# Graph attention on one core: DVE turns half of the mask tiles of the last two row chunks, and ACT and POOL take over the sums at two borders

## The reference

```
h  = maximum(layernorm(x), 0)                # x [4096, 128]
Wh = h @ W;  a1, a2 = a[:128, 0], a[128:, 0]
e  = (Wh @ a1)[:, None] + (Wh @ a2)[None, :]
e  = where(e > 0, e, 0.2 * e)
e  = where(adj > 0, e, -9e15)                # adj [4096, 4096] int32, 64 MB
out = x + elu(softmax(e, axis=1) @ Wh)
```

## Time and profile before

| | |
|---|---|
| time, median of 3 runs (lowest to highest) | 244.91 us (244.35 to 244.97) |
| profiled execution: its own time, its span | 244.79 us, 243.0 us |
| busy share of the span: PE, PEld, DVE, ACT, POOL | 93%, 91%, 81%, 64%, 24% |
| granted TensorE clock, mean | 0.982 of full speed |
| DMA: moved, mean rate | 71.92 MB, 296 GB/s |

### The profile page before, as it was taken

The page is one execution under the profiler, slowest core; times in us unless marked ns, Lnnn a source line. Parts: engine busy times, 40 slices in busy tenths (PEclk is TensorE's granted clock), DMA queues, the critical chain, the costliest instruction groups (busy, mean ns, idle before and its releaser), DMA issues.

```text
span 243.0 us, 8254 instructions
## 1 busy us (share of the span) xinstructions
PE 227.0 (93%) x3736; PEld 221.2 (91%) x3736; DVE 196.4 (81%) x259; ACT 156.2 (64%) x139; POOL 59.1 (24%) x48
## 2 busy tenths in 40 slices
PE   6969999599999999999999999999999999999970
PEld 2759899599998999999999999999999999999970
DVE  4999997536776998889887988898879888998864
ACT  3698836697799999944996677019975774000051
POOL 3648036897000070300000560000001710040000
PEclk9997999999999999999999999999999999999995
DMA  6999999999998999999999999999999300020002
GB/s 225 360 389 386 386 386 385 388 367 370 301 352 284 363 395 386 388 385 385 398 386 385 388 385 385 385 387 369 386 386 386 140 0 3 3 89 3 3 0 92
DMA packets 36521, 71.92 MB, mean 296 GB/s; under 512 B 1282, under 2 KB 1924, under 8 KB 36484
## 3 DMA queue, kind: packets, MB, share of 16 engines
q1 hardware_dynamic: 35520, 69.74, 79.0%
q10 hardware_dynamic: 964, 1.64, 1.8%
HBM read 69.27 MB, written 2.10 MB: 294 GB/s over the span
## 4 chain that ended last, share of the span: by engine, by line
PE 74%; ACT 8%; DVE 7%; issue 4%; POOL 4%; DMA 1%; ACTq 0%; DVEq 0%; POOLq 0%
PE acc L834 20%; PE acc L835 20%; PE acc L836 20%; PE mask_t L817 11%; ACT mask L420 4%; POOL v L330 2%; POOL val L333 2%; ACT neg L432 1%; DVE words L610 1%; DVE stats L547 1%; DMA x_sb<-in_x_dram 1%; PE acc L796 1%; PE acc L805 1%; ACT neg L511 1%; DVE wh_sb L573 1%
## 5 line engine op out<-in xcount | busy, mean ns | idle before, releaser
L610 DVE SCALAR_TENSOR_TENSOR words<-g_row,gq_word,mask_t 128x1024 f32<-128x1024 f32 x128 | 161.4, 1278 | 36.0 <-PE acc L836 19.0
L834 PE MATMUL acc<-val,words 128*128 128x129 f16 x1000 | 171.9, 220 | 0.3 <-DVE wh_sb L573 0.3
L835 PE MATMUL acc<-val,words 128*128 128x129 f16 x1000 | 171.9, 220 | 0.0
L836 PE MATMUL acc<-val,words 128*128 128x129 f16 x1000 | 171.9, 220 | 0.0
L420 ACT ACTIVATE mask<-raw,step_bias 128x2048 uint8<-128x2048 int32 x63 | 121.8, 1993 | 28.4 <-DVE x_sb L626 17.3
L834 PEld LDWEIGHTS acc<-val,words 128*128 128x128 f16 x1000 | 97.8, 98 | 0.5 <-issue 0.5
L835 PEld LDWEIGHTS acc<-val,words 128*128 128x128 f16 x1000 | 97.9, 98 | 0.1
L836 PEld LDWEIGHTS acc<-val,words 128*128 128x128 f16 x1000 | 97.8, 98 | 0.0
L817 PE MATMUL mask_t<-ident_b,mask 128*128 128x128 bf16 x512 | 34.3, 221 | 1.8 <-ACT mask L420 1.8
L817 PEld LDWEIGHTS mask_t<-ident_b,mask 128*128 128x128 bf16 x512 | 30.3, 99 | 2.2 <-ACT mask L420 2.2
L358 POOL TENSOR_TENSOR hp<-num,rz 128x1024 f32<-128x1024 f32 x3 | 5.7, 1897 | 105.3 <-DVE rz L621 105.3
(11 more groups left out here) (91 smaller groups left out, 125.4 us busy)
## 6 DMA issues: line engine op xcount, KB each, us to landing
raw<-in_adj_dram SPq DMA_DIRECT2D x64, 1024.0 KB, 14.1
x_sb<-in_x_dram SPq DMA_DIRECT2D x8, 256.0 KB, 5.7
out_dram<-x_sb ACTq DMA_DIRECT2D x3, 512.0 KB, 7.9
out_dram<-x_sb SPq DMA_DIRECT2D x2, 128.0 KB, 2.4
out_dram<-x_sb SPq DMA_DIRECT2D x1, 192.0 KB, 1.9
w_sb<-in_L_gnn_W_dram ACTq DMA_DIRECT2D x1, 64.0 KB
out_dram<-x_sb SPq DMA_DIRECT2D x1, 64.0 KB, 1.6
a_sb<-in_L_gnn_a_dram ACTq DMA_DIRECT2D x1, 1.0 KB
```

Source lines behind the costliest of these rows:

```text
L610: nc.vector.scalar_tensor_tensor(words[:, q], g_row[:, c * CHUNK:(c + 1) * CHUNK], gq_word[:, 1, t:t + 1], maskt_bytes[:, u % 2, q // 2, : ...
L834: nc.tensor.matmul(acc_tile(t), high, val[:, tile, 0, 0:V], start=first and t % PT == 0, stop=False, skip_group_check=True)
L835: nc.tensor.matmul(acc_tile(t), high, val[:, tile, 1, 0:V], start=False, stop=False, skip_group_check=True)
L836: last = nc.tensor.matmul(acc_tile(t), low, val[:, tile, 0, 0:V], start=False, stop=False, skip_group_check=True)
```

## The change

**DVE turns.** In chunks 2 and 3 the columns of units 4 to 7 (columns 2048 to 4095, here called a set) go another way. A set's 1024 x 2048 numbers come in four loads of 2 MB; load h holds 256 rows of it. A quarter of the partitions (32) holds these rows with 512 of the columns, so a load is four DMAs of 512 KB, each to 32 partitions: SP issues those of quarters 0 and 1, and ACT those of quarters 2 and 3 (`load_set` on both). ACT makes bytes of them into pair buffers (`set_to_bytes`), and one DVE instruction, `transpose` of 128x1024 words of four bytes in squares of 32, turns a unit (`turn_set`). It writes `mask_t` in a layout in which a byte of four belongs to each q. The 16 transposes on PE fall away for these eight units. DVE turns a unit ahead of the last step of the unit before.

**Order.** In these chunks the units run in the order 0, 1, 4, 2, 5, 3, 6, 7, and the loads in the order unit 0, set load 0, set load 1, unit 1, set loads 2 and 3, units 2 and 3 (`LOADS`). Unit 4, in third place, needs all four set loads. `mask` has two slots in these chunks, as the other two are a pair buffer.

**Values.** The columns of a turned set lie on other partitions, so SP moves the value tiles of the second half with 16 DMAs of 80 KB from SBUF to SBUF (`move_values`, four behind each of loads 18 to 21). DVE writes the word of each column beside the value tiles (`split_weights_sums`, two small copies more), and POOL clears that space once at the start. Row tiles of chunks 2 and 3 are in linear order; their rows of `x` are loaded a second time, 1 MB, behind load 26 (`load_rows`, after PE has ended chunk 1).

**Borders.** For chunks 1 and 2 ACT reads the sums from PSUM (`take_sums` on ACT, three copies), standing in ACT's order behind loads 19 and 28, which are the fourth load of chunk 2 and the fifth of chunk 3. POOL adds the seed, and DVE only takes the reciprocal (`invert`). For all borders POOL and ACT do the rest, and `result` falls away from DVE. Of the four DMAs of the last output three are left.

The core of the diff:

```diff
+    SETS = C - 2
+    ORDER = [[*range(U)] if c < SETS else [0, 1, 4, 2, 5, 3, 6, 7] for c in range(C)]
+    LOADS = [(c, u, None) for c in range(SETS) for u in range(U)]
+    for c in range(SETS, C):
+        LOADS += [(c, 0, None), (c, None, 0), (c, None, 1), (c, 1, None), (c, None, 2), (c, None, 3), (c, 2, None), (c, 3, None)]
...
+            def load_set(at):
+                c, _, h = LOADS[at]
+                for k in SP_QUARTERS:
+                    sp.dma_start(raw[k * QUARTER:(k + 1) * QUARTER, at % RING], adj_set[c, 1, h, k]).then_inc(set_in[at % RING], 16)
+            def move_values(k):
+                for m in range(4):
+                    sp.dma_start(val_set[k * QUARTER:(k + 1) * QUARTER, 4 * m:4 * m + 4],
+                                 val[m * QUARTER:(m + 1) * QUARTER, (4 + k) * BT:(5 + k) * BT]).then_inc(val_moved, 16)
...
-            sp.dma_start(out_v[C - 1, :, 0, 3:4], last[:, 3:4]).then_inc(out_done, 16)
-            sp.dma_start(out_v[C - 1, :, 1, 0:2], last[:, 4:6]).then_inc(out_done, 16)
...
+            for at in range(1, C * U):
+                if LOADS[at][1] is None:
+                    sp.wait_ge(act_bytes, 2 * (at - RING) + 1)
+                    load_set(at)
...
+                if 18 <= at < 22:
...
+                    move_values(at - 18)
+                if at == 26:
+                    sp.wait_ge(words_free, SETS * U * BT)
+                    sp.wait_ge(val_moved, MOVES * 16)
+                    load_rows(C - 2)
+                    load_rows(C - 1)
...
             def tail(c):
+                if c >= 1:
+                    pool.wait_ge(acc_free, 3 * c + 3)
+                    nc.gpsimd.tensor_tensor(num[:], num[:], seed_row[:].unsqueeze(1).broadcast_to([P, CT, V]), ALU.add).then_inc(seeded, 1)
                 pool.wait_ge(rz_ready, c + 1)
...
+            def set_to_bytes(c, h):
+                at = LOADS.index((c, None, h))
+                act.wait_ge(set_in[at % RING], 64 * FILLED[at])
...
+            def load_set(at):
+                if at < C * U and LOADS[at][1] is None:
+                    c, _, h = LOADS[at]
+                    act.wait_ge(act_bytes, 2 * (at - RING) + 1)
+                    for k in ACT_QUARTERS:
+                        act.dma_start(raw[k * QUARTER:(k + 1) * QUARTER, at % RING], adj_set[c, 1, h, k]).then_inc(set_in[at % RING], 16)
+            def take_sums(c):
+                if c >= 2:
+                    act.wait_ge(hp_ready, c + 1)
+                for k, (t0, t1) in enumerate(BANKS):
+                    wait_bank(act, c, k)
+                    nc.scalar.copy(num[:, t0:t1], acc_bank(k)).then_inc(acc_free, 1)
...
+            for at in range(U, C * U):
+                c, u, h = LOADS[at]
+                if u is None:
+                    set_to_bytes(c, h)
+                else:
                     for k in range(2):
                         to_bytes(c, u, k)
+                load_set(at + RING)
+                if at == 13:
+                    tail(0)
+                if at == 15:
+                    store(0)
+                if at == 19:
+                    take_sums(1)
+                if at == 22:
+                    tail(1)
+                if at == 26:
+                    store(1)
+                if at == 28:
+                    take_sums(2)
+            tail(2)
+            store(2)
...
+            def turn_set(c, i):
+                m = ORDER[c][i] - 4
+                if m == 0:
+                    dve.wait_ge(act_bytes, 2 * LOADS.index((c, None, 3)) + 1)
+                dve.wait_ge(words_ready, 4 * (c * U + i - 1))
+                nc.vector.transpose(maskt_quads[:, i % 2].rearrange("p (t h r) -> p t h r", h=4, r=QUARTER),
+                                    pair_quads[PAIRS[c][m // 2]][:, m % 2]).then_inc(set_turned, 1)
...
+                        if q == BT - 1 and u < U - 1 and is_set(c, ORDER[c][u + 1]):
+                            turn_set(c, u + 1)
                         weights(c, u, q)
-                        if (u, q) == (0, 2):
-                            take_sums(c - 1)
-                        if (u, q) == (4, 3):
-                            result(c - 1)
+                        if c == 1 and (u, q) == (0, 2):
+                            take_sums(0)
+                        if c >= 2 and (u, q) == (1, 1):
+                            invert(c - 1)
...
+            def turn_ahead(c, i):
+                if i == U - 1:
+                    c, i = c + 1, -1
+                if not is_set(c, ORDER[c][i + 1]):
+                    turn(c, i + 1)
```

More of the change, by code:

```diff
@@ L48, in bass_graph_attention @@
     U = NB
+    SETS = C - 2
[3 more added lines that the diff above has]
+        LOADS += [(c, 0, None), (c, None, 0), (c, None, 1), (c, 1, None), (c, None, 2), (c, None, 3), (c, 2, None), (c, 3, None)]
+    FILLED = [len([b for b in range(a % RING, a + 1, RING) if (LOADS[b][1] is None) == (LOADS[a][1] is None)]) for a in range(C * U)]
     V = F + 1
@@ L155, in turned_bank, with rows_of, is_set, turning @@
             return mask_t[:, 1, b % 2, :]
+        def rows_of(c):
+            if c < SETS:
+                return x_sb[:, group(c)]
+            t0 = T * VP // 2 + (c - SETS) * CHUNK
+            return val_f32[:, t0:t0 + CHUNK].rearrange("p (t f) -> p t f", f=F)
+        def is_set(c, u):
+            return c >= SETS and u >= 4
+        def turning(c, u):
+            if c < SETS:
+                return c * U + u + 1, c * U + u + 1 - RING
+            i = SETS * U + (c - SETS) * 4 + u
+            return i + 1, i + 1 - (RING if i < SETS * U + 2 else 2)
+        def mask_slot(c, u):
+            return u % RING if c < SETS else u % 2
         x_in = [sem(f"x_in{b}") for b in range(NB)]
@@ L159, in bass_graph_attention @@
         raw_in = [[sem(f"raw_in{s}_{k}") for k in range(2)] for s in range(RING)]
+        set_in = [sem(f"set_in{i}") for i in range(RING)]
+        set_turned = sem("set_turned")
+        pad_clear = sem("pad_clear")
+        pad_ready = sem("pad_ready")
+        val_moved = sem("val_moved")
+        rows_in = [sem(f"rows_in{c}") for c in range(C)]
+        seeded = sem("seeded")
         first_bytes = sem("first_bytes")
@@ L414, in to_bytes @@
             def to_bytes(c, u, k):
[L415 to L420, removed]
-                                     scale=1.0, bias=step_bias[:, 0:1]).then_inc(act_bytes, 1)
+                at = LOADS.index((c, u, None))
@@ L816, in turn, with value_tile, product @@
                     for t in range(CT):
-                        last = nc.tensor.transpose(maskt_pairs[:, u % 2, h, t * P:(t + 1) * P], mask_pairs[:, u % RING, t, :, h], ident_b[:])
+                        last = nc.tensor.transpose(maskt_pairs[:, i % 2, h, t * P:(t + 1) * P],
+                                                   mask_pairs[:, mask_slot(c, u), t, :, h], ident_b[:])
                 last.then_inc(turned, 1)
-            def product(c, u, q):
-                n = c * U + u
-                first = (u, q) == (0, 0)
+            def value_tile(c, i, q):
+                u = ORDER[c][i]
+                return val_set[:, (u - 4) * BT + q] if is_set(c, u) else val[:, u * BT + q]
+            def product(c, i, q):
+                n = c * U + i
+                first = (i, q) == (0, 0)
                 pe.wait_ge(words_ready, 4 * n + q + 1)
-                tile = u * BT + q
+                if is_set(c, ORDER[c][i]):
+                    pe.wait_ge(val_moved, MOVES * 16)
+                v = value_tile(c, i, q)
                 for t in range(CT):
@@ L833, in product @@
                     low = words_h[:, q, t * P:(t + 1) * P, LO]
[L834 to L837, removed]
+                    nc.tensor.matmul(acc_tile(t), high, v[:, 0, 0:V], start=first and t % PT == 0, stop=False, skip_group_check=True)
+                    nc.tensor.matmul(acc_tile(t), high, v[:, 1, 0:V], start=False, stop=False, skip_group_check=True)
+                    last = nc.tensor.matmul(acc_tile(t), low, v[:, 0, 0:V], start=False, stop=False, skip_group_check=True)
+                    if (i, q) == (U - 1, BT - 1) and t in (2, 5):
                         last.then_inc(acc_done, 1)
@@ L906, in _ @@
                 if u == U - 1:
-                    turn(0, u + 1)
+                    turn_ahead(0, u)
                 for q in range(BT):
@@ L930, in _ @@
                     else:
-                        turn(c, u + 1)
+                        turn_ahead(c, u)
                         for q in range(BT):
```

174 lines of the change are left out of this document (115 added, 59 removed).

## The result

The changed kernel takes 286.0 us (median of 4 runs, 283.7 to 292.1) where the kernel before takes 244.7. The forecast was 240.6, with a range up to 257. The change is slower by 40, outside the range and on the other side. The profiled execution took 283.7, with a span of 281.9.

What follows compares the result with a forecast made beforehand. PE was taken to bound the kernel, with DMA having little room. From 244.8: PE turns -7.1, first border +1.0, second border +2.3, end -0.6, start +0.2, giving 240.6 us, range 236.8 to 257.

Steps and rivals of the forecast that it cites:

- How fast is a quarter load?: Set loads to 32 partitions each: taken at the full 386 GB/s of plain loads, named as the outweighing unknown.
- rival A: Quarter loads are slow, paid at the second border: 258 if half their bytes move at half rate, 276 if all; chance 0.36.
- The moves: Value moves ahead of load 28: 1.31 MB, with 1.05 MB of x rows 6.1 us of DMA time together.
- PE: Chunks 2 and 3: eight units lose their turn of 0.89, -7.1 us; products stay 5.44 a unit.
- DVE: Four transposes more a chunk, 1.2 us of pitch each; 43.1 a chunk, under PE's 47.1 and 46.2, cost 0.
- ACT at the first border: Start of chunk 2: ACT converts unit 2 late after taking the sums, so PE waits +1.0 us (0 to 2).
- Second border: Start of chunk 3: load 28 lands at 180.8, ACT reads sums behind it, PE waits +2.3 us (0 to 5.0).
- Start, borders and end: Clear and small copies at start at most +0.2; work taken from DVE at borders worth nothing; fewer output DMAs -0.6 us.
- The sum: Whole kernel: 244.8 - 7.1 + 1.0 + 2.3 - 0.6 + 0.2 = 240.6 us.

Runs made afterwards that it cites:

- e3: Kernel before, with units 4 to 7 of chunks 2 and 3 loaded as four 512 KB DMAs to 32 neighbouring partitions each, all on SP: 258.7 us, ratio 1.056.
- e4: Kernel before, loads cut as in e3, but each DMA to every fourth partition instead of 32 neighbours: 244.8 us, ratio 1.001.
- e1: Changed kernel, with each set load's four 512 KB DMAs going to all 128 partitions, on the same two queues: 253.4 us, ratio 1.035 to the kernel before.
- e7: As e3 on the kernel before, but eight 256 KB DMAs a load, quarters in the order 0, 2, 1, 3: 247.7 us, ratio 1.012.
- e9: Whole change, set loads as eight alternating 256 KB DMAs on SP, moves alternating and behind loads 8 to 11: 274.2 us (all four runs: median 281.6, ratio 1.150).
- e8: As e3 on the kernel before, but two 1 MB DMAs a load, to partitions 0 to 63 and 64 to 127: 258.6 us, ratio 1.056.
- e5: e1 without the 16 value moves and their waits; set units use the value tiles of units 0 to 3: 240.4 us, ratio 0.982 to the kernel before.
- e11: Changed kernel without sets or value moves, keeping borders on ACT and POOL and three DMAs at the end: 243.8 us, ratio 0.996 to the kernel before.
- e6: e1 with value moves of the same size, from and to every fourth partition instead of 32 neighbours: 246.2 us, ratio 1.006 to the kernel before.

## Why the prediction was wrong, step by step

**The step that failed** stands under "How fast is a quarter load?": "I take the full rate: two queues feed both halves of the partitions together, and only the partitions differ from a plain load." Only the partitions differ, and that alone makes them slow. e3 against e4 shows it without anything else of the change: 218 and 386 GB/s, 258.7 and 244.8. Two queues don't repair it: in the changed kernel, with SP on one half and ACT on the other, the rate is 261 to 275 in stretches that hold plain loads too, and putting full loads in their place gives back 31.4 us (e1). Nor is it that both queues are seldom in step alone, since e7 and e9, which alternate inside one queue, stay at 237 to 303.

The Trainium skill had this rule (SBUF — State Buffer, the table in the section "Door 1: The DMA port swizzle"): 32 and 64 neighbours from 0 reach half of the ports (the ways by which DMA gets into SBUF) and level off at about 218 GB/s. e3 and e8 agree, with 218 and 217 to 223. The Trainium skill says too (same page, section "Can I just issue two DMAs to hit both halves?") that two concurrent DMAs to the two halves gain only 6%. Here eight alternating ones gain 20% (e7, 261 to 218), more than that and far from double. The prediction quoted the rule and gave it the smaller chance because no row bore on it; that was the wrong way to weigh it, as no row bore against it either.

**The price of rival A** was named as 258 or 276, one for one at the second border from 35 us of set loads. The cause is right, the path only in part, and the size too small: 284.8. Up to load 28 there are seven set loads (17, 18, 20, 21, 25, 26, 28) and not six and a half, and ACT starts on 28 when all of it has landed: 38 us, by which the two prices are 260 and 279. At 218 GB/s in place of 386 they lose 29, for 270, and the prediction's own six and a half 27, for 268, where it wrote "above 270". The measured 31.4 (e1) is of that size, but PE loses 10.4 and 5.1 us before 190, where the prediction had the loads in time, and at the second border it waits longer for load 27 than for the sums behind 28.

The moves are what was missing: costed at 3.4 by their bytes, they cost 13.0 (e1 to e5). Both numbers hold the price of a lower clock: the span is 43.3 longer than that of e5, but PE stands only 37.6 - 2.7 = 34.9 longer, and most of the other 8 is PE working at the lower clock, of which below.

**What held.** *PE:* 24 turned units and 5.44 a set. *DVE:* 1.25 for a transpose (1.2 taken, as pitch), and in e5 no hole on PE from DVE's work but one of 0.6 before the last unit. *ACT at the first border:* +1.0 forecast, and PE's hole in e5 at 146 to 150 is 4.00 - 2.96 = 1.04. *Second border:* +2.3 forecast, 2.00 - 0.42 = 1.6 in e5. *Start, borders and end:* forecast -0.4 (0.2 - 0.6) together, and e11 is -1.0 (-0.5 to -1.5 by its interval): nothing at the borders, and a little more gained than forecast. *The sum:* 240.6, and e5, which has all of the change but the two things I mis-sized, takes 240.4. The match is luckier than it looks: without the moves the second border of the sum would be 0, for 238.3, where e5 has 1.6 there. The turning by DVE is worth 243.8 - 240.4 = 3.4 (e11 to e5). From matmul start to matmul start, e5's new holes are 1.5 at the first border, 1.7 at the second and 0.6 before the last unit, and 7.1 - 3.8 = 3.3 is nearly all of it.

**The account**, each step one edit: 284.8 changed kernel; -31.4 loads to all partitions (e1); -7.2 spread moves (e6); -5.8 no moves (e5); 240.4. Against 244.7 before, the idea itself gains 4.3, and the way its data is brought in place costs 44.4. Each price holds in this order of steps.

No kernel of these that leaves nothing out beats the kernel before. What this way of turning needs, a quarter of the columns on 32 neighbouring partitions, was loaded in just the form in which DMA is slow, one quarter a DMA, and DMA has only its lead to give: in e7 the loads end at about 213 instead of 191 and the time is already 2.9 longer, with nothing yet spent on moves or rows.

**What stays open.** The slow form lies in the cut into DMAs, and the data can end in the same places by another cut: DMAs to every fourth partition, which takes eight of each quarter, and the same for the moves. Such DMAs are fast (386 GB/s in e4, 389 with the moves of e6), but in these runs they bring other data than the turn needs, and no run tried it with that data. What is shown to fail is this way of loading. With both cut so, an estimate is e6's 246.2, still not under 244.7, since the moves' bytes and the longer wait for the sums remain.

## What to carry to other kernels

Give each DMA partitions from the whole range, not 32 or 64 neighbours: when a layout asks for neighbours, price its bytes at 218 GB/s instead of 386 before anything else. Read the rate, not the busy share, to see whether DMA has room, and count the lead (how long ahead of its use a load lands) as a budget that late loads overdraw one for one. Ask of every late load which plain loads stand behind it in the queue, and who needs those first. Where the Trainium skill has a measured rule for a form that the trace doesn't hold, one run of the old kernel with only that form is cheaper than an argument.

## What the runs showed of the hardware that was not expected

*The clock behind a hole.* In the changed kernel PE stops at about 135, and the granted clock falls from 1.00 to 0.50 (2.4 to 1.2 GHz):

```profile
140.00:145.00 5.00, 0.00 (x0) 0.00 (x0) 0.00 (x0) 1.91 (x2) 0.00 (x0) 0.50 1.07 226
145.00:150.00 5.00, 4.86 (x46) 4.86 (x47) 0.26 (x1) 1.70 (x5) 2.19 (x1) 0.50 1.07 225
150.00:155.00 5.00, 5.00 (x90) 5.00 (x89) 3.66 (x4) 3.32 (x2) 1.90 (x1) 0.99 1.07 226
```

PE works again from 145 on, but at half pace: 46 matmuls in 5 us instead of 90. So a hole costs more than its length, here about 2.5 us. Holes of 1.0 and 1.6 (e5) left the clock at 1.00; behind the 4.1 of e6 it was 0.87 from 190 to 200.

*Small moves inside SBUF.* 16 DMAs of 80 KB cost 13.0 us of time. To neighbouring partitions they slow the loads beside them (283 GB/s in all instead of 387); to spread ones they don't (389), and cost 5.8.

*POOL.* One instruction with two operations (`max`, then `add`) over 128x1024 took 3.63, where the kernel before had 2.78 for one with a single operation. It costs nothing: e11 has it too, and no hole on PE.
